# Consecutive tokens in the passes for the maxima, and another way for the maxima into the row of shifts

## The reference, cut to what matters

```python
x: (4, 1024, 256)        # batch, tokens, width; 16 heads of 64
q = jnp.einsum('bnd,hde->bhne', query, Wq) * scale
k = jnp.einsum('bmd,hde->bhme', query, Wk)
v = jnp.einsum('bmd,hde->bhme', query, Wv)
logits = jnp.einsum('bhne,bhme->bhnm', q, k)
attn = jax.nn.softmax(logits, axis=-1)
out = jnp.einsum('bhnm,bhme->bnhe', attn, v)
```

## Time and profile before

| | |
|---|---|
| median of three runs | 2046.39 us |
| profiled execution, its own time | 2046.98 us |
| its span in the trace | 2045.3 us |
| TensorE busy | 1932.6 us, 94% |
| GpSimd busy | 1366.8 us, 67% |
| VectorE busy | 1320.6 us, 65% |
| ScalarE busy | 914.5 us, 45% |
| last pass starts | 1691.1 us |

### The profile page before, as it was taken

One profiled execution on the slowest core, in us unless ns is written; L12 is line 12 of the kernel. 1 busy time (PEld: TensorE's weight loads), 2 busy tenths in 40 slices (PEclk: granted clock), 3 DMA queues, 4 the chain that ended last, 5 costly groups with the idle time before them and its releaser, 6 DMA issues. The chain is left out here.

```text
span 2045.3 us, 30646 instructions
## 1 busy us (share of the span) xinstructions
PE 1932.6 (94%) x11400; PEld 1282.6 (63%) x11400; DVE 1320.6 (65%) x2187; ACT 914.5 (45%) x1182; POOL 1366.8 (67%) x725
## 2 busy tenths in 40 slices
PE   7999999999999999899999998999999997777996
PEld 5565566556666656556665665566666553777886
DVE  5566666666666666867666668676666667454454
ACT  3444444444434454344445443344344533445663
POOL 1787777778657776797667766786677767353453
PEclk9999999999999999999999999999999998877999
DMA  4200000012111100022102000211111101621330
GB/s 152 73 21 17 22 16 22 21 45 86 48 37 46 34 21 17 19 80 84 37 27 63 16 22 17 66 44 47 37 46 34 32 11 47 211 86 65 124 115 32
DMA packets 150094, 104.24 MB, mean 51 GB/s; under 512 B 74044, under 2 KB 136636, under 8 KB 148924
## 3 DMA queue, kind: packets, MB, share of 16 engines
q1 hardware_dynamic: 146876, 93.82, 15.4%
q0 software_dynamic: 3072, 8.46, 1.1%
HBM read 69.15 MB, written 29.43 MB: 48 GB/s over the span
## 5 line engine op out<-in xcount | busy, mean ns | idle before, releaser
L937 POOL TENSOR_TENSOR prob_sum<-prob_sum,probs 128x1024 f32<-128x1024 f32 x384 | 924.8, 2408 | 228.4 <-ACT probs L1146 186.8
L1210 DVE TENSOR_REDUCE max_of<-spare_ps 128x1 f32<-128x512 f32 x1024 | 656.2, 682 | 353.2 <-PE spare_ps L1029 351.8
L1146 ACT ACTIVATE probs<-score_ps 128x1024 f32<-128x1024 f32 x512 | 516.0, 1027 | 533.9 <-PE score_ps L1050 526.2
L1064 PE MATMUL av_ps<-probs,v 128*64 128x512 f32 x2048 | 470.2, 601 | 5.0 <-issue 4.5
L1029 PE MATMUL spare_ps<-k_hi,q_hi 64*128 64x512 f32 x1024 | 293.7, 560 | 30.6 <-DVE max_of L1210 24.0
L1064 PEld LDWEIGHTS av_ps<-probs,v 128*64 128x64 f32 x2048 | 140.2, 137 | 272.3 <-issue 257.0
L1029 PEld LDWEIGHTS spare_ps<-k_hi,q_hi 64*128 64x128 f32 x1024 | 166.9, 306 | 228.2 <-issue 217.9
L933 POOL TENSOR_TENSOR prob_sum<-probs 128x1024 f32<-128x1024 f32 x64 | 153.3, 2396 | 196.9 <-ACT probs L1146 196.9
L1221 DVE RECIPROCAL sums<-sums 128x128 f32<-128x128 f32 x256 | 233.5, 932 | 28.3 <-ACT sums L1158 28.3
L1050 PE MATMUL score_ps<-q_hi,k_hi 64*128 64x512 f32 x1024 | 215.8, 401 | 1.3 <-DVE o_in L1234 0.9
L1050 PE MATMUL score_ps<-shift_rows,one_rows 64*128 64x512 f32 x1024 | 212.4, 396 | 0.0
(11 more groups left out here) (201 smaller groups left out, 2371.6 us busy)
## 6 DMA issues: line engine op xcount, KB each, us to landing
o_transposed<-o_out SPq DMA_DIRECT2D x64, 256.0 KB, 2.1
w_raw<-in_L_ffn_W_dram SPq DMA_DIRECT2D x16, 1024.0 KB, 5.5
o_in<-o_transposed SPq DMA_DIRECT2D x26, 512.0 KB, 4.0
w_raw<-in_L_attn_Wq_dram SPq DMA_DIRECT2D x64, 64.0 KB, 2.3
w_raw<-in_L_attn_Wk_dram SPq DMA_DIRECT2D x64, 64.0 KB, 2.2
wv_raw<-in_L_attn_Wv_dram SPq DMA_DIRECT2D x32, 128.0 KB
x<-in_x_dram SPq DMA_DIRECT2D x4, 1024.0 KB, 5.7
xT_kept<-x_transposed SPq DMA_DIRECT2D x4, 1024.0 KB, 7.1
```

The source lines that it names most:

```text
L937: pool.tensor_tensor(out, out, probs[:, n % RING], ALU.add).then_inc(prob_added, 1)
L1064: last = pe.matmul(av_ps[hd * E:(hd + 1) * E, :], v[:, quad % 2, kt, 2 * first_head + hd, :], probs[:, n % RING, hd, :], start=(kt == 0), ...
L1146: act.activation(probs[:, n % RING], score_ps[n % 2][:, :, :], ACT.Exp).then_inc(probs_ready, 1)
L1210: dve.tensor_reduce(max_of[:, u % 2, kh, j, hd:hd + 1], bank[:, :], AX.X, ALU.max).then_inc(pass_read, 1)
```

## The change

Four things go together.

1. `row_pass`: `j` now picks 128 consecutive tokens, j*128 to j*128 + 127 of the unit's 512. The weights of a pass are 128 neighbours in each partition where they were every fourth.
2. `read_pass`: partition p, column (head, j) of `neg_max` now holds token 128j + p. `neg_max` becomes a [128, 32] tile, its columns 8 to 31 zeroed once; VectorE writes columns 0 to 7, waits for itself (`max_found`), and transposes the tile in four blocks of 32x32 into `neg_rows`. There partition 32r + 4 head + j holds the tokens 128j + 32r to 128j + 32r + 31 in 32 neighbouring columns. Both tiles have one place, not two: the transpose waits for the transfer of the unit before, where the reduction waited for the transfer of two units before.
3. `move_shift`: four DMAs, one for each block r, each from 8 partitions of 128 bytes to eight pieces of 128 bytes in `shift_rows`; `shift_in` counts 64 for a unit where it counted 32.
4. The ones are held in one tile for both uses; GpSimd fills it over a corner of `prob_sum` at the start and waits once for `rows_set`.

```diff
@@ row_pass
-                tokens = slice(u % 2 * BANK + j, (u % 2 + 1) * BANK, JT)
+                tokens = slice(u % 2 * BANK + j * P, u % 2 * BANK + (j + 1) * P)
@@ read_pass, after the eighth pass
                     dve.wait_ge(pass_read, n + 2)
-                    wait(dve, shift_in[u % 2], 32 * (u // 2))
-                    dve.tensor_reduce(neg_max[:, u % 2, :, :], max_of[:, u % 2].rearrange("p k j h -> p h j k"),
-                                      AX.X, ALU.max, negate=True).then_inc(max_done, 1)
+                    dve.wait_ge(max_zeroed, 1)
+                    dve.tensor_reduce(neg_max[:, 0:2 * JT].rearrange("p (h j) -> p h j", j=JT),
+                                      max_of[:, u % 2].rearrange("p k j h -> p h j k"),
+                                      AX.X, ALU.max, negate=True).then_inc(max_found, 1)
+                    dve.wait_ge(max_found, u + 1)
+                    wait(dve, shift_in[(u - 1) % 2], 64 * ((u + 1) // 2))
+                    dve.transpose(neg_rows[:, :].bitcast(F32), neg_max[:, :].bitcast(F32)).then_inc(max_done, 1)
@@ move_shift
-                for hd in range(2):
-                    sp.dma_start(shift_rows[hd * E:hd * E + 1, u % 2, :].rearrange("a (q j) -> a q j", j=JT).bitcast(F32),
-                                 neg_max[:, u % 2, hd, :].bitcast(F32)).then_inc(shift_in[u % 2], 16)
+                for r in range(P // BLOCK):
+                    rows = neg_rows[r * BLOCK:r * BLOCK + 2 * JT, :]
+                    heads = shift_rows[0:E + 1:E, u % 2, :].rearrange("h (j r i) -> h r j i", j=JT, i=BLOCK)
+                    sp.dma_start(heads[:, r].bitcast(F32), rows.bitcast(F32)).then_inc(shift_in[u % 2], 16)
@@ score
-                    pe.wait_ge(shift_in[u % 2], 32 * (u // 2 + 1))
+                    pe.wait_ge(shift_in[u % 2], 64 * (u // 2 + 1))
@@ tiles
-        neg_max = sb("neg_max", [P, 2, 2, JT], F32R)
+        neg_max = sb("neg_max", [P, BLOCK], F32R)
+        neg_rows = sb("neg_rows", [P, BLOCK], F32R)
-        one_rows = sb("one_rows", [P, P], F32R)
@@ gpsimd, start
-            pool.memset(ones[:, :], 1.0).then_inc(rows_zeroed, 1)
+            pool.memset(neg_max[:, :].bitcast(F32), 0.0).then_inc(max_zeroed, 1)
+            pool.memset(prob_sum[:, 0, 0, 0:P], 1.0).then_inc(rows_zeroed, 1)
             pool.memset(o_out[:, :, :], 0.0).then_inc(rows_zeroed, 1)
             pool.wait_ge(rows_zeroed, 2)
-            pool.tensor_copy(one_rows[:, :], ones[:, :]).then_inc(rows_set, 1)
+            pool.tensor_copy(one_rows[:, :], prob_sum[:, 0, 0, 0:P]).then_inc(rows_set, 1)
             pool.tensor_copy(shift_rows[:, :, :], o_out[:, :, :]).then_inc(rows_set, 1)
+            pool.wait_ge(rows_set, 2)
```

More of the change, by code:

```diff
@@ L25, in build_constants @@
     ident = ctx.enter_context(nc.sbuf_tensor("ident", [P, P], F32))
-    ones = ctx.enter_context(nc.sbuf_tensor("ones", [P, P], F32))
+    ones = ctx.enter_context(nc.sbuf_tensor("ones", [P, P], F32R))
     ident_zeroed = ctx.enter_context(nc.semaphore("ident_zeroed"))
@@ L45, in __init__ @@
         self.oT_dram, self.xe_dram = oT_dram, xe_dram
-        self.ident, _, _, self.ones = const
+        self.ident, _, _, ones = const
+        self.ones = ones[:, :].bitcast(F32)
         self.CC = CC = oT_dram.shape[1]
@@ L637, in build_attention @@
     PIECES = 4
+    BLOCK = 32
     assert 2 * E == P and KT == 8 and SCALE == 0.125 and N == 2 * BANK
-    ident, ident_zeroed, ident_ready, ones = const
+    ident, ident_zeroed, ident_ready, one_rows = const
+    ones = one_rows[:, :].bitcast(F32)
     BITES = list(FIRST_BITES)
@@ L781, in build_attention @@
         pass_read = sem("pass_read")
+        max_zeroed = sem("max_zeroed")
+        max_found = sem("max_found")
         max_done = sem("max_done")
```

## The result

The changed kernel took 2024.26 us (median of four runs, 2021.36 to 2028.11) against 2046.76 us (2043.78 to 2048.28) for the kernel before on the same chip: a ratio of 0.9893, 95% interval 0.987 to 0.9916. It is faster by 22.5 us where 37.2 had been forecast, and lies 0.26 us above the range. A second measurement on another chip gave 2022.77 us, ratio 0.987 (0.9841 to 0.9899). The profiled run took 2021.85 us, its span is 2020.1: 25.2 us less than before.

The account below looks back on a forecast made before the run. TensorE was taken to bound the attention stage, with exposed pass loads; 45.4 - 1.4 - 4.8 - 2 = 37.2 us off 2047.0 gave 2009.8 (2009.2 from the median), forecast 2009. Range 1997 to 2024, the forecast's own 1999 to 2018.

Parts of the forecast that it names:

- The load: Passes on TensorE: 378 exposed weight loads each get 0.12 us shorter with consecutive tokens, 45.4 us gained.
- The signs: Expected: load 186 to 200 ns, mean pass matmul about 470, step behind values' product 0.33 us, round 1.41 us.
- The start and VectorE's bursts: 12 early passes gain nothing (1.4 us back); passes at about 20 waits in routing bursts only wait longer (4.8 back).
- Transfers: Two DMAs become four between maxima and scores: hidden before and after, 0 us.
- The transposition: VectorE, one in each of 64 units, 0.25 us with its wait, mostly absorbed: 2 us lost, ends 0 and 16.
- my two signs of a wrong forecast: Load stays near 300, or it falls and TensorE's idle before the pass, released by VectorE, grows over 15 us.
- Rival 1: VectorE takes the load's place: transposes half on the path, half the passes behind 700 us gain nothing; 2026 us, 16%.
- Rival 2: The stride isn't what makes the pass's load long: no gain, 2049 us, or 2047 if transposes are hidden; 3%.
- Rivals 3 and 4: 3: transposition dear, 0.93 us each, 2061 us, 3%. 4: shorter load hidden too, 1960, or partly 1992, 6%.

Follow-up runs that it names:

- e1: Changed kernel without the transposition, negated maxima written straight into neg_rows, all transfers kept: 2010.99 us, ratio 0.9791 to the kernel before.
- e3: Changed kernel with the transposition issued two pass readings later in even units: 2011.77 us, ratio 0.98 to the kernel before.
- e2: Changed kernel with a pass's weights taken from every fourth token again, transposition and four DMAs kept: 2066.26 us, ratio 1.0062 to the kernel before.
- e8: Kernel before with the maximum over the experts' logits taken twice in each batch: 2054.71 us, ratio 1.0023 to the kernel before.
- e10: Changed kernel with later transposition, two reciprocals one step later and VectorE's choice of experts behind a pass's reading: 2013.85 us, ratio 0.9819 to the kernel before.
- e4: Changed kernel with two reciprocals of the fourth row of steps each one step later: 2009.64 us, ratio 0.9784 to the kernel before.

## Why the prediction fell short

**The load, 45.4 us: right.** 0.12 us, from a score behind the same values' product, was the price: steps of 458 to 461 ns became 337, and steps of 430 to 434 became 305 to 310. 336 passes were exposed in that way where I counted 378 from mean durations, which gives 41.5 us; with smaller gains at the others the passes' steps gave 43.2. The signs came as named: load 185 ns, mean matmul 469, step 0.34, round 1.42 to 1.44 against 1.41. (The starts that I gave for the round before, 1003.39 and 1004.95, are 1.56 apart and not 1.54, and 1.56 - 0.12 is the 1.44 measured.)

**The start and VectorE's bursts, 1.4 and 4.8 us: right in sum.** Without the transposition the gain is 2045.3 - 2008.2 = 37.1 us (e1), or 41 by the medians on e1's chip, where the forecast's sum without that term was 37.2 + 2 = 39.2. How much of it each of the two terms is, no run separates.

**Transfers, 0: right.** No wait for `shift_rows` appeared, and the kernels of e1 and e3 have all four DMAs.

**The transposition, 2 us: this is the step that failed; it measured 12** in the spans, and more by the ratios (e1). Its own length was right (0.25 us with its wait, as estimated; 211 ns alone), and 12 lies within the ends of 0 and 16 that I gave. What it delays was wrong in two ways.

- I wrote that in half the units a reciprocal or two scores follow, "which gives room". It is the other way round. In the even units the burst of reading, maxima, reciprocal, reading, reciprocal, reading has no idle time, and pass B waits for its middle: 5.7 us in 27 units. In the odd ones, where the reductions follow at once, a projection absorbs nearly all of it, as I said. (My 1.75 us for those is 1.71: 1.29 + 0.17 + 0.25.) The rows of the VectorE timeline at 327.01 to 331.36 us of the kernel before show the burst; I had read the plain rounds at 1005 us only the earlier trace rows, and took the earlier trace rows's 24 waits as belonging to the routing.
- The choice of experts stands behind the same burst, and its subtraction led GpSimd's addition by only 0.03 us. 0.21 us more and it waits the addition out: 5.5 us in three places. I had costed GpSimd as an engine with room, not as one that can block VectorE.

That leaves about 1 us of the 12. It lies at least in part in the odd units, where the step from the eighth pass to the next is 0.03 us shorter in e1 (1.44 us against 1.47, the mean of twelve between 60 and 700 us).

Neither of my two signs of a wrong forecast came: the load fell to 185 ns, and the idle time before the pass put down to VectorE grew by 13.6 us, not by over 15. The second was set too high, since it was above the 12 us that were enough to leave the range. The last pass, which I put near 1652 us, started at 1666.8.

**The rivals.** Rival 1's 2026 was nearest in number, but half of its sum was wrong: the passes behind 700 us kept their gain. Its other half, the transpositions partly on the path at 8 us, is what happened, and larger, but not by its mechanism: e3 keeps all of VectorE's work and loses nothing, so VectorE hasn't taken the load's place as the bound. Rival 2 (the stride isn't the cause) is refuted by e2. Rivals 3 and 4 did not occur. The chance of faster, 0.94, was right; the range's upper end of 2024 left out half of the case that came true, since rival 1's 2026 lay outside it.

## What to carry to other kernels

An instruction added to an engine that is a third idle costs what it delays in the one place where that engine has no idle time and another waits: look for the densest burst in front of a wait, not at the mean load, and put the instruction behind it. If it must stand there, look for VectorE operations on operands in SBUF that start just ahead of a GpSimd addition, since a quarter of a microsecond can turn 0.23 us into 2.3. Weights of fp32 taken with a stride of 16 bytes load in 306 ns where neighbours take 185, which is worth a new layout when the load is exposed.

## What the runs showed of the hardware

- A VectorE subtraction of 128x64 with both operands in SBUF takes 0.23 us when it starts before GpSimd's 128x1024 addition, and until that addition's end when it starts after it (2.28, 2.25 and 1.28 us in the changed kernel, e8 and e10). Which operation is hit changes from kernel to kernel with shifts of 0.2 us.
- A VectorE operation with one input (TENSOR_SCALAR, 128x8) took 2.40 us instead of 0.17 inside such additions in e4, so two inputs are not needed for it.
- 128 fp32 weights in 64 rows load in 185 ns from neighbours, 191 with a stride of 8 bytes and 306 with a stride of 16.
- A 128x32 fp32 transposition takes VectorE 211 ns; what is queued behind it starts 0.25 us later.
